# Attention, linear attention, LSTM and FP4 FFN in one kernel: another order of work in the first stage's steps

## Chip, cores and metric

The kernel runs on one core of one Trainium2 chip. The metric is device time in microseconds: before the change the median of three runs is 953.55 us (952.65 to 953.72).

## What is computed

The input x has 64 sequences of 64 rows of 256. The first stage computes x1 = x + attention part, the second x1 + FFN part:

```python
# first stage, per sequence
y  = softmax_attention([image key; k], [image value; v], q) @ c_proj   # 16 heads of 16, causal, one extra key
q2, k2, v2 = relu(y @ Wq.T + bq), relu(y @ Wk.T + bk), y @ Wv.T + bv
ctx = (q2 @ (k2.T @ v2)) / max(q2 @ sum(k2), 1e-6)                     # per head
x1  = x + layernorm(ctx + y) * gamma + beta
# second stage
hs  = lstm(x1, h0=cond, Wx, Wh, b)                                     # along the 64 rows
out = x1 + fp4_linear(silu(fp4_linear(hs, w_gate)) * fp4_linear(hs, w_up), w_down)
```

Most products are done as three f16 products of a high and a low part (high x high, high x low, low x high). So each operand of such a product is made twice: a cast on ScalarE gives the high part, and a subtraction on VectorE the low part.

## The kernel before

**Tiles and steps.** A tile is two sequences, 128 rows, so there are NT = 32 of them. The first stage is a software pipeline written out by hand: each engine has its own function `step`, and `pipeline` calls it with a list of tiles, the newest first (t1 = tile n, t2 = tile n-1, and so on). Step n of an engine does the early work of t1 and later work of t2 to t5. Steps 0 to 9 are written out, steps 10 to 29 are a loop of ten rounds with two steps each, and the rest is written out again. Each engine carries out its list in order; semaphores join them. The second stage (LSTM, FP4 products) follows from about 514 us on and is not changed.

**What a step does.** For t1: x's high and low part (of the tile after it), the q, k product (`qk`), the split of q and k into `qk16` (L1104 to L1107 on ScalarE, L1376 and L1377 on VectorE), their DMA transposes into `qkT` (L555), the scores of the first eight heads (`scores(t1, 0)`, L827) and the mask sum `masked(t1, 0)` (L1347). For t2: the scores of the other eight heads, row maxima (`maxima`, L1355), subtraction of them (`shift`, L651, GpSimd), exp (L1082), p's high part (L1088) and low part (`probs_lo`, L658), the image key's part (`image_part`, L667), and the transposes of p (`probs_turn`, L540). For t3: p times v (`attend`, L841), the sum of the parts and its division (L1387 to L1396), the transpose of the result (onT), the projection y (L1163), y's transpose and yT's high and low part (L1077, L1331). For t4: the linear attention (`linear_q`, `linear_kv`, `outer`, `linear_out`; L1403 to L1421), the residual (L711), and the statistics: `bn_stats` (L1445), `bn_aggr` (L1453), variance plus epsilon (L713) and rstd (L715). For t5: z (L1137), times gamma (L685), plus x and beta (L692) which gives x1, its high part (L1156) and low part (L1433), the DMA transposes of x1 (L574) and its store (L576).

**SyncE's queue.** All DMAs are issued from SyncE, in order. In a step these are: on even steps x_in for the next pair (L547); the two q, k transposes (L555); p's two transposes (L540); on even steps the image values of two tiles (L568, two issues of 136 KB); x1's transposes and store (L574, L576); on even steps x_res (L579). An issue whose source isn't ready holds up all behind it.

**VectorE's order.** A step begins with maxima of t2's first heads, then x's low part, the split of q and k, weight work in steps 0 to 8 (`chore`), the second mask sum and maxima of t2, the sum and division of t3, the head mask of t4 (L1403), onT's low part, ctx (L1421), v's low part (L1428), x1's low part (L1433), the mask sum of t1 (L1347), statistics of t4 (L1445), yT's low part (L1331), and the aggregation (L1453). In the last steps of the stage the weights of the FFN are split too (`ffn_hi`, `ffn_lo`, L483).

**Helpers.** `hold(engine, semaphore, value, passed)` waits and then increments a counter; `after` is a wait that is left out where its value isn't positive. All matrix products with three parts are on L783.

## Time and profile before

| | before |
|---|---|
| median of 3 runs | 953.55 us (952.65 to 953.72) |
| the profiled execution | 955.28 us, span 953.6 us |
| mean granted TensorE clock | 0.926 |
| TensorE (PE) busy | 766.9 us, 80% |
| VectorE (DVE) busy | 747.1 us, 78% |
| ScalarE (ACT) busy | 429.5 us, 45% |
| GpSimd (POOL) busy | 436.2 us, 46% |
| DMA, mean 93 GB/s | 89.04 MB, queue q1 46.7% of 16 engines |
| issue to landing, median: q, k transposes | 4.2 us |
| issue to landing, median: image values (32 issues of 136 KB) | 3.1 us |

The span runs from the first to the last instruction of the profiled execution, and the difference to 955.28 us lies around it. Busy shares are means over two stages with different limits; the page gives them in 40 slices of 23.8 us, of which slices 3 to 21 are about the first stage. A number in brackets behind a row of a timeline is the idle time of the engine before the operation, and what ended it.

### The profile page before, as it was taken

Reading aid. Unit: us, or ns where it says so; the run is one execution under the profiler, and the core shown is the slowest. Engines: PE = TensorE matmul, PEld = TensorE weight load, DVE = VectorE, ACT = ScalarE, POOL = GpSimd, SP = SyncE. Lnnn points to the kernel's source line nnn. Section 1 sums busy time; section 2 is a strip of 40 time slices with the busy share of each in tenths; the row PEclk is TensorE's granted clock in tenths of the full one; section 3 lists DMA queues with packets and bytes.
Section 4 is the critical chain, followed back from the end, with each engine's and each line's share of the span. In section 5 each row is a group of like instructions: output and inputs, shape, how many; then the busy total and the mean of one; then the engine's idle time right before and its main releaser. Section 6 shows DMA issues by size and latency. Waiting matters only on the chain.

```text
span 953.6 us, 23040 instructions
## 1 busy us (share of the span) xinstructions
PE 766.9 (80%) x7494; PEld 466.0 (49%) x7494; DVE 747.1 (78%) x1773; ACT 429.5 (45%) x1145; POOL 436.2 (46%) x596
## 2 busy tenths in 40 slices
PE   3347677778888778887767799999999999999965
PEld 1124454445455444554444455555555556555633
DVE  6177878667777778777744689999999999999883
ACT  2054656556665666665553333333333333333320
POOL 0054777666766667766742033322233333222332
PEclk9767989889998999999898999999999999999987
DMA  5965656676665666666620023323332333233332
GB/s 120 185 168 98 113 112 105 124 130 132 131 128 122 133 127 139 132 138 127 119 56 23 17 48 59 66 58 67 64 64 59 67 59 64 60 66 64 65 64 63
DMA packets 262383, 89.04 MB, mean 93 GB/s; under 512 B 233266, under 2 KB 261298, under 8 KB 262325
## 3 DMA queue, kind: packets, MB, share of 16 engines
q1 hardware_dynamic: 262324, 88.25, 46.7%
q8 instruction: 39, 0.64, 0.3%
q14 instruction: 20, 0.16, 0.1%
HBM read 25.19 MB, written 8.47 MB: 35 GB/s over the span
## 4 chain that ended last, share of the span: by engine, by line
PE 29%; DVE 17%; POOL 11%; issue 10%; SPq 9%; DMA 6%; ACT 4%; POOLq 0%; DVEq 0%; ACTq 0%
PE bank L783 10%; PE bank L920 8%; PE bank L931 5%; DVE x_value L170 4%; DMA qkT<-qk 4%; SPq L540 3%; POOL p L658 2%; DVE ffn_room L1530 2%; DVE ffn_room L1526 2%; POOL prob L651 2%; PE bank L1000 2%; PE bank L911 2%; POOL zg_rows L685 1%; SPq L568 1%; POOL x_rows_sb L692 1%
## 5 line engine op out<-in xcount | busy, mean ns | idle before, releaser
L783 PE MATMUL bank<-gu,xqT 128*128 128x512 f16 (+1 forms) x576 | 128.5, 371 | 8.6 <-DMA xqT<-xq_split 8.6
L729 POOL TENSOR_TENSOR ffn_room<-prob,h_coarse 128x704 f16<-128x704 f32 x32 | 44.1, 1377 | 154.4 <-DVE prob L171 154.4
L920 PE MATMUL bank<-wx,x1T 128*64 128x512 f16 x768 | 97.9, 392 | 2.9 <-DMA x1T<-x_split 2.9
L931 PE MATMUL bank<-wh,h 128*64 128x512 f16 x768 | 96.0, 386 | 0.7 <-ACT h L1190 0.7
L651 POOL TENSOR_TENSOR prob<-prob,row_max 128x520 f32<-128x520 f32 x64 | 68.8, 1075 | 50.7 <-DVE row_max L1355 50.7
L783 PEld LDWEIGHTS bank<-gu,xqT 128*128 128x128 f16 x576 | 56.2, 102 | 69.2 <-issue 12.2
L920 PEld LDWEIGHTS bank<-wx,x1T 128*64 128x64 f16 x768 | 79.4, 203 | 13.5 <-DMA x1T<-x_split 3.7
L1009 PE MATMUL bank<-dn,hqT 128*128 128x256 f16 x576 | 70.0, 277 | 7.6 <-DMA hqT<-ffn_room 6.6
L658 POOL TENSOR_TENSOR p<-prob,p 128x512 f16<-128x512 f32 x64 | 72.0, 1125 | 1.2 <-ACT p L1088 1.2
L1009 PEld LDWEIGHTS bank<-dn,hqT 128*128 128x128 f16 x576 | 54.7, 99 | 26.5 <-issue 18.3
L931 PEld LDWEIGHTS bank<-wh,h 128*64 128x64 f16 x768 | 41.5, 111 | 42.0 <-issue 12.1
L1347 DVE TENSOR_TENSOR prob<-bank,add_mask 128x260 f32<-128x260 f32 x128 | 48.4, 419 | 16.5 <-PE bank L827 16.2
L154 ACT ACTIVATE qk<-prob 128x704 bf16<-128x704 f32 x32 | 25.3, 792 | 75.5 <-DVE prob L167 75.5
L827 PE MATMUL bank<-qkT 64*64 64x65 f16 x1024 | 22.6, 211 | 45.7 <-DMA qkT<-qk 32.4
L783 PE MATMUL bank<-attn,xT 128*128 128x512 f16 x192 | 59.1, 454 | 0.0
L783 PE MATMUL bank<-yT,lin 128*128 128x128 f16 x384 | 31.1, 239 | 34.4 <-DVE yT L1331 34.4
L811 PE MATMUL bank<-attn,xT 128*64 128x256 f16 x768 | 56.8, 287 | 0.0
L1082 ACT ACTIVATE prob<-prob 128x520 f32<-128x520 f32 x64 | 40.7, 635 | 30.9 <-POOL prob L651 30.9
L724 POOL TENSOR_TENSOR h_coarse<-h_scale,one_h 128x44 bf16<-128x44 f32 x32 | 8.9, 279 | 98.3 <-DVE h_scale L165 98.3
L788 PE MATMUL bank<-bias_rows_sb,ones_bf 96*128 96x512 bf16 (+1 forms) x96 | 36.7, 383 | 18.3 <-DVE onT L1331 9.8
L783 PE MATMUL bank<-lin,yT 128*128 128x512 f16 x192 | 50.7, 403 | 0.0
L783 PEld LDWEIGHTS bank<-yT,lin 128*128 128x128 f16 x384 | 26.5, 109 | 48.3 <-DVE yT L1331 40.5
(193 smaller groups left out, 1869.5 us busy)
## 6 DMA issues: line engine op xcount, KB each, us to landing
vimg_in<-image_values SPq DMA_DIRECT2D x32, 136.0 KB, 3.1
x_in<-in_x_columns SPq DMA_DIRECT2D x16, 256.0 KB, 2.9
x_res<-in_x SPq DMA_DIRECT2D x16, 256.0 KB, 3.0
x_rows<-x_rows_sb SPq DMA_DIRECT2D x32, 128.0 KB, 1.8
ffn_room<-x_rows SPq DMA_DIRECT2D x64, 64.0 KB, 2.2
out<-ffn_room SPq DMA_DIRECT2D x64, 64.0 KB, 2.0
add_mask<-in_mask_Bx1x1xS_ff SPq DMA_DIRECT2D x2, 512.0 KB, 7.6
qkT<-qk SPq DMA_TRANSPOSE x64, 4.2
```

The lines of the kernel that those rows point to most:

```text
L170: 5: lambda: dve.scalar_tensor_tensor(out=v, in0=mag, scalar=1.25 * MAGIC, in1=v, op0=ALU.max, op1=ALU.subtract),
L651: pool.tensor_tensor(prob[:, r, :], prob[:, r, :], row_max[:, r, None].to_broadcast([P, 8, KEYS]), ALU.subtract).then_inc(s["shifted"], 1)
L658: pool.tensor_tensor(p16[:, r, 1, :], prob[:, r, 0:S], p16[:, r, 0, :], ALU.subtract).then_inc(s["p_lo"], 1)
L729: pool.tensor_tensor(blocks(hq_split[:, 0], FF), blocks(fp4_h.value, FF), spread(h_coarse, FF), ALU.mult).then_inc(s["hq_hi"], 1)
L783: last = pe.matmul(dst, lhs(a, c), rhs(b, c), start=first and c == 0 and a == b, stop=c == C - 1 and (a, b) == parts3[-1], skip_group_chec ...
L788: pe.matmul(dst, ones_bf[:, :], bias_bf[name][:, lo:hi], start=True, stop=False, skip_group_check=True)
L811: last = pe.matmul(bank[3][64 * copy:64 * copy + 64, D * h:D * h + D], xT16[:, t.parity, a, P * c + 64 * h:P * c + 64 * h + 64], attn16[:, ...
L920: last = pe.matmul(bank[e][B * h:B * h + B, :], x1T16[m][:, c, :, at], half_cols(wx16, a, c, h), start=False, stop=True, skip_group_check= ...
L931: last = pe.matmul(bank[e][B * h:B * h + B, :], h16[:, m, c, :], half_cols(wh16, a, c, h), start=False, stop=True, skip_group_check=True)
L1009: last = pe.matmul(dst, hqT16[:, t.parity, a, k, :], dn16[:, m, k, :], start=k == 0 and (a, m) == (0, 0), stop=k == FFC - 1 and a == 1, sk ...
L1082: act.activation(prob[:, r, :], prob[:, r, :], ACT.Exp, scale=1.0 / SCORE).then_inc(s["probs"], 1)
L1347: last = dve.tensor_tensor(prob[:, at:at + 4, :], bank[side][:, 0:4 * KEYS].rearrange("p (r k) -> p r k", k=KEYS), add_mask[:, bass.ds(t.n ...
```

## The change

All of it is in the first stage. The pipelines of VectorE and SyncE get a sixth tile, t6.

- SyncE: the image values go tile by tile (`image_values`, two issues of 68 KB a step in place of two of 136 KB on even steps) and stand first in the step; x_res is next (now for t4 of even steps), then x_in, then the q, k transposes, then x1's transposes and store (of t6), and last p's transposes.
- VectorE: yT's low part stands ahead of the mask sum of t1, and the maxima of that sum follow it in the same step (before: first thing of the next). Statistics come a step later (t5), behind x's low part, and the aggregation behind the split of q and k, with three counted waits (`passed`). x1's low part comes a step later (t6), behind the second maxima.
- GpSimd: variance and rstd (t5) stand behind the copy of the image keys; x1's sum (L692) stands behind p's low parts.
- ScalarE: onT's high part stands ahead of the second exp; x1's high part (L1156) behind yT's.

```diff
@@ SyncE
+        def image_values(t):
+            hold(sp, s["img_part"], t.count(2, 2, back=2), "sp_passed")
+            for b in range(2):
+                sp.dma_start(vimg_in[64 * b:64 * b + 64, t.parity].rearrange("p h c -> p (h c)"),
+                             vimg_sides[b][t.number()].partition_broadcast(S)).then_inc(vimg_loaded, 16)
         def step(tiles):
-            t1, t2, t3, _, t5 = tiles
+            t1, t2, _, t4, _, t6 = tiles
+            if t1 and (t1.loop is not None or t1.b > 0):
+                image_values(t1)
+            if t4 and t4.parity == 0:
+                after(sp, s["xb_ready"], t4.count(back=1))
+                sp.dma_start(x_res[:, :, :], x_pairs[t4.pair()]).then_inc(xres_loaded, 16)
...
-            if t2:
-                probs_turn(t2, 0)
-                probs_turn(t2, 1)
...
-                if t1.parity == 0:
-                    hold(sp, s["img_part"], t1.count(2, 2, back=1), "sp_passed")
-                    for b in range(2):
-                        sp.dma_start(vimg_in[64 * b:64 * b + 64, :].rearrange("p j h c -> p j (h c)"),
-                                     vimg_sides[b][bass.ds(t1.number(), 2)].partition_broadcast(S)).then_inc(vimg_loaded, 16)
...
-            if t5:
-                hold(sp, s["x1_lo"], t5.count(), "sp_passed")
+            if t6:
+                hold(sp, s["x1_lo"], t6.count(), "sp_passed")
...
-            if t3 and t3.parity == 0:
-                after(sp, s["xb_ready"], t3.count(back=1))
-                sp.dma_start(x_res[:, :, :], x_pairs[t3.pair()]).then_inc(xres_loaded, 16)
-        pipeline(sp, 5, step, first=10)
+            if t2:
+                probs_turn(t2, 0)
+                probs_turn(t2, 1)
+        pipeline(sp, 6, step, first=10)
@@ GpSimd
+            if t5:
+                pool.wait_ge(s["mean_ready"], t5.count())
+                after(pool, s["rstd_ready"], t5.count(back=1))
+                after(pool, s["z_ready"], t5.count(back=1))
+                pool.tensor_tensor(var_eps[:, :], mean_var[:, 1:2], eps_ln[:, :], ALU.add).then_inc(s["var_ready"], 1)
+                pool.wait_ge(s["var_ready"], t5.count())
+                pool.tensor_tensor(rstd[:, :], var_eps[:, :], neg_half[:, :], ALU.pow).then_inc(s["rstd_ready"], 1)
             if t2:
                 image_part(t2, 0)
                 shift(t2, 1)
...
                 pool.tensor_tensor(zg_rows[:, :], z_rows[:, :], gamma_sb[:, :], ALU.mult).then_inc(s["zg_ready"], 1)
+            if t2:
+                probs_lo(t2, 0)
+                image_part(t2, 1)
+                probs_lo(t2, 1)
             if t5:
...
                 pool.tensor_tensor(x1_rows[:, t5.parity, :], zg_rows[:, :], xb_rows[:, :], ALU.add).then_inc(s["x1_ready"], 1)
-            if t2:
-                probs_lo(t2, 0)
-                image_part(t2, 1)
-                probs_lo(t2, 1)
@@ ScalarE
                 probs_hi(t2, 0)
-                exp(t2, 1)
             if t3:
                 hi(t3, onT16[:, 0, :], bank[0][:, 0:D], "onT_ps", "onT_hi", "y_ps")
+            if t2:
+                exp(t2, 1)
@@ VectorE
+        def passed(sem, value):
+            hold(dve, sem, value, "dve_passed")
         def step(tiles):
-            t1, t2, t3, t4, t5 = tiles
+            t1, t2, t3, t4, t5, t6 = tiles
-            if t2:
-                maxima(t2, 0)
             if t1 and (t1.loop is not None or t1.b < NT - 1):
                 x_lo(Tile(t1.loop, t1.b + 1))
+            if t5:
+                dve.wait_ge(s["resid"], t5.count())
+                dve.bn_stats(stats[:, :], res_rows[:, :]).then_inc(s["stats_ready"], 1)
...
+            if t5:
+                passed(s["stats_ready"], t5.count())
+                passed(s["var_ready"], t5.count(back=1))
+                passed(s["neg_ready"], t5.count(back=1))
+                dve.bn_aggr(mean_var[:, :], stats[:, :]).then_inc(s["mean_ready"], 1)
             chore(t1, 0)
             if t2:
                 masked(t2, 1)
                 maxima(t2, 1)
+            if t6:
+                dve.wait_ge(s["x1_hi"], t6.count())
+                dve.tensor_tensor(x1_split[:, 1, :], x1_rows[:, t6.parity, :], x1_split[:, 0, :], ALU.subtract)\
+                    .then_inc(s["x1_lo"], 1)
...
-                masked(t1, 0)
-            if t4:
-                dve.wait_ge(s["resid"], t4.count())
-                dve.bn_stats(stats[:, :], res_rows[:, :]).then_inc(s["stats_ready"], 1)
...
             if t3:
                 lo(t3, yT16[:, 1, :], bank[6][:, D:2 * D], yT16[:, 0, :], "yT_hi", "yT_lo")
+            if t1:
+                masked(t1, 0)
+            if t1:
+                maxima(t1, 0)
             if t4:
-                dve.bn_aggr(mean_var[:, :], stats[:, :]).then_inc(s["mean_ready"], 1)
                 ffn_lo(t4, "mean")
```

## Rows read from the trace of the kernel before

**Rows 1.** By stretch: us (instructions) of PE, PEld, DVE, ACT, POOL; clock, DMA, GB/s

```profile
322.00:348.00 26.00, 20.86 (x283) 13.04 (x283) 19.89 (x54) 16.11 (x42) 17.91 (x27) 0.93 0.64 131
```

**Rows 2.** SyncE's queue: start, us, line, operation, what; q, k issues, steps 3, 10, 31

```profile
82.93 1.29 SPq L555 DMA_TRANSPOSE qkT<-qk  x1
...
188.15 3.34 SPq L555 DMA_TRANSPOSE qkT<-qk  x2
...
462.80 3.04 SPq L555 DMA_TRANSPOSE qkT<-qk  x2
```

**Rows 3.** SyncE's queue over one pair of steps

```profile
308.91 3.02 SPq L555 DMA_TRANSPOSE qkT<-qk  x2
...
320.44 3.19 SPq L555 DMA_TRANSPOSE qkT<-qk  x2
326.83 2.87 SPq L540 DMA_TRANSPOSE pT<-p  x2
330.00 1.49 SPq L568 DMA_DIRECT2D vimg_in<-image_values  x2
331.80 1.23 SPq L574 DMA_TRANSPOSE x1T<-x_split  x1
333.22 0.44 SPq L576 DMA_DIRECT2D x_rows<-x_rows_sb  x1
333.94 0.40 SPq L579 DMA_DIRECT2D x_res<-in_x  x1
334.67 1.29 SPq L555 DMA_TRANSPOSE qkT<-qk  x1
```

**Rows 4.** VectorE in order of time, same pair; in brackets idle time before, and releaser

```profile
319.75 0.41 DVE L1377 TENSOR_TENSOR qk<-bank,qk 128x256 f16<-128x256 f32 x1
...
321.48 0.44 DVE L1387 TENSOR_TENSOR bank<-bank,o_img 128x272 f32<-128x272 f32 x1
...
326.98 1.35 DVE L1433 TENSOR_TENSOR x_split<-x_rows_sb,x_split 128x256 f16<-128x256 f32 x1
...
329.63 0.43 DVE L1445 BATCH_NORM_STATS2 stats<-res_rows 128x6 f32<-128x256 f32 x1 [0.62 <-POOL res_rows L711]
330.09 0.42 DVE L1331 TENSOR_TENSOR yT<-bank,yT 128x256 f16<-128x256 f32 x1
...
331.43 0.42 DVE L1376 TENSOR_TENSOR qk<-bank,qk 128x256 f16<-128x256 f32 x1
...
332.09 0.76 DVE L1347 TENSOR_TENSOR prob<-bank,add_mask 128x260 f32<-128x260 f32 x2
332.88 0.69 DVE L1355 TENSOR_REDUCE row_max<-prob 128x8 f32<-128x520 f32 x1
333.50 0.45 DVE L1387 TENSOR_TENSOR bank<-bank,o_img 128x272 f32<-128x272 f32 x1
```

**Rows 5.** TensorE in order of time, same pair of steps

```profile
315.03 0.44 PE L827 MATMUL bank<-qkT 64*64 64x65 f16 x16 [2.32 <-DMA qkT<-qk]
...
326.49 0.32 PE L827 MATMUL bank<-qkT 64*64 64x65 f16 x16
327.04 0.44 PE L849 MATMUL bank<-ident,y_rows 128*128 128x128 f32 x2 [0.23 <-ACT y_rows L1163]
...
330.57 0.84 PE L783 MATMUL bank<-yT,lin 128*128 128x128 f16 x12 [1.58 <-DVE yT L1331]
```

**Rows 6.** GpSimd in order of time: the low part of p beside x1's low part

```profile
326.93 1.12 POOL L658 TENSOR_TENSOR p<-prob,p 128x512 f16<-128x512 f32 x1
```

**Rows 7.** VectorE and GpSimd in step 31, the other order of starts

```profile
467.50 0.44 DVE L1433 TENSOR_TENSOR x_split<-x_rows_sb,x_split 128x256 f16<-128x256 f32 x1
...
467.62 1.30 POOL L658 TENSOR_TENSOR p<-prob,p 128x512 f16<-128x512 f32 x1
```

**Rows 8.** VectorE at the stage's end: the last weight splits

```profile
509.61 0.95 DVE L483 SCALAR_TENSOR_TENSOR gu<-bank,gu 128x512 f16<-128x512 f32 x2
```

**Rows 9.** p's transposes (L540): time from issue to landing over the whole trace

```profile
DMA to landing us min/median/max: 3.0/3.2/4.8
```

More of the change, by code:

```diff
@@ L1164, in step @@
                 hi(t3, yT16[:, 0, :], bank[6][:, D:2 * D], "yT_ps", "yT_hi", "kv2_ps")
+            if t5:
+                act.wait_ge(s["x1_ready"], t5.count())
+                after(act, s["x1T_in"], t5.count(per=16, nth=16, back=1))
+                act.copy(x1_split[:, 0, :], x1_rows[:, t5.parity, :]).then_inc(s["x1_hi"], 1)
             ffn_hi(t4, "mean")
@@ L1460, in _ @@
         x_lo(Tile(None, 0))
-        pipeline(dve, 5, step, first=10)
+        pipeline(dve, 6, step, first=10)
         dve.memset(hq_split[:, :, FF:], 0.0).then_inc(s["b_zero"], 1)
```

27 lines of the change are left out of this document (6 added, 21 removed).

## The prediction

> **What bounds the kernel now.** I read the page first (busy shares by slice), then the busy times by stretch, then SyncE's DMA queue in order of time, then VectorE, TensorE, GpSimd and ScalarE over the same two steps. In the steady part of the first stage no engine is full: in 26 us TensorE works 20.9, VectorE 19.9, GpSimd 17.9, ScalarE 16.1 [rows 1]. What counts is the waits that end last. The second stage (from 514 us on) is not touched and keeps its time.
>
> A step handles one new tile and older ones behind it. Steps come in pairs, since x_in and x_res move two tiles at once. From the q, k transposes issued at 188.15 us (step 10) to those at 462.80 us (step 31) there are 21 steps in 274.65 us [rows 2]: 26.16 us a pair. In the pair shown they go out at 308.91, 320.44 and 334.67 us [rows 3]: 11.53 and 14.23 us apart. I call the issue at 320.44 that of an even step, those at 308.91 and 334.67 odd. Two waits stand out:
>
> Wait one, the queue. In the long step q and k are split from 331.43 us on, 0.66 us from there to the next operation [rows 4], so they are ready at about 332.2, but the transposes leave at 334.67: SyncE first issues p's transposes, the image values, x1's transposes, x1's store and x_res [rows 3]. 2.5 us late. In the same place a pair earlier the lateness shows as TensorE idle: the scores at 315.03 waited 2.32 us for qkT [rows 5].
>
> Wait two, yT's low part. TensorE waits 1.58 us for it before 330.57; y's transposes were done by 327.5 [rows 5]. VectorE is first busy with x1's low part (1.35 us) and the mask sum and then sits 0.62 us idle ahead of the statistics, which wait for GpSimd's residual [rows 4].
>
> **The change part by part.** A "gap" is start to start on one engine. I write s for the start of the scores of the new tile's first half on TensorE (326.49 in the even step) and run one step of the new order from it.
>
> (a) yT's low part first. y's transposes begin at s+0.55 and take 0.44 [rows 5]; ScalarE's cast behind them I take at 0.4, as VectorE's operation on the same tile has 0.42 [rows 4]. Low part at s+1.45. Linear q can then start right behind the next q, k product: wait two is gone. Price: the mask sum begins about 1 us after its scores, not at once.
>
> (b) VectorE from there: yT's low part 0.34 (the two operations of the split, of the same size, have gaps of 0.33), mask sum 0.79, maxima 0.62, x's low part 0.34, statistics 0.46, split done 0.75 later [rows 4]: s+4.75. The statistics' residual was made a step before, so the 0.62 us of idleness has no cause left. SyncE issues 0.28 us after the split (319.75+0.41 to 320.44) [rows 3, 4]: s+5.0.
>
> (c) From that issue to the scores it takes 315.03-308.91 = 6.12 us [rows 3, 5]. **Loop one**: 5.0+6.1 = 11.1 us a step.
>
> (d) x1's low part comes a step later, behind the second maxima. It takes 1.35 us [rows 4] where GpSimd's p low part started 0.05 us before it, and it ends 0.28 after that one's end [rows 6]; 0.44 where it started first, with GpSimd's at 1.30 in place of 1.12 [rows 6, 7]. In the new place the operation behind the maxima starts 0.62 us after their start [rows 4], GpSimd's subtraction only after their end at 0.69 plus a semaphore: VectorE should be first by some 0.1 to 0.2 us. I take a gap of 0.34; bounds 0.34 and 1.35.
> The Trainium skill (SBUF — State Buffer, Who interferes with whom) says that a VectorE instruction with two inputs in SBUF and a GpSimd one that reads SBUF exclude each other for the whole instruction, the first to start having it. The rows named before this agree; by this rule the part is unhindered when first, and when second it waits out GpSimd's whole subtraction.
>
> (e) **Loop two**: split 0.66 from s+4.0, aggregation 0.2 (estimate, a tiny operation), second mask sum 0.79, maxima 0.62, x1's part 0.34 put the sum with the image part at s+6.6. From that operation to the next scores it is 326.49-321.48 = 5.0 us now [rows 4, 5], less 0 to 0.5 because onT's high part no longer stands behind an exp on ScalarE: 11.1 to 11.6, I take 11.35. VectorE is then close to full: 19.9/2 us [rows 1] less about 1 for x1's part leaves it 9 to 10 of 11.4.
>
> (f) The three "passed" counters ahead of the aggregation are waits that are met, each with an increment. SyncE has three like them in the 0.33 us between x_res's end and the q, k issue [rows 3]: so 0 to 0.3 us here, taken as inside the 11.35.
>
> (g) SyncE's queue, by gaps [rows 3]: x1's transposes 1.42, its store 0.72, p's 3.17, image values 1.80, x_res 0.73, x_in taken alike, q, k transposes 3.3 (3.19 and a semaphore). The image values go from two issues a pair to four, of half the bytes. Bytes seem to count little (two of 136 KB take 1.49, one x_res of 256 KB 0.40), so I take 1.80 again; bounds 1.0 and 1.8. Odd step 3.3+1.42+0.72+3.17+1.80 = 10.4 us, below the loops. Even step 10.4+1.46 = 11.9, above them: this is what is late next. Behind the waits: x_in waits for x's low part (s+3.2) with q and k behind it, which want s+5.0: no loss. x1's transposes wait for x1's low part, done at s+6.6, 1.6 us after the q, k issue and before its 3.3 us are over: no loss. p's are now last, 5.4 us behind the q, k issue.
>
> (h) GpSimd: variance and rstd move from the step's end, where they waited for the aggregation, to its middle; x1's sum goes behind p's low parts, so these come about 0.9 us sooner. rstd again waits for the aggregation (s+4.9), with the image part and second subtraction behind it; these want an exp and the maxima of about s+5 and s+5.9: hidden, 0.5 if not. The residual ends near s+13.4 (estimate) and is wanted a step later at s+14.5: 1 us to spare.
>
> (i) ScalarE: onT's high part ahead of the second exp delays that exp by 0 to 0.4 us, off both loops. x1's high part fits behind yT's.
>
> **Sum.** A pair is 11.9 (queue) + 11.35 (loop two) = 23.25 for 26.16: 2.91 us, times 10.5 pairs = 30.6 us. The steps from 3 to 10 (82.93 to 188.15 us, 15.0 each [rows 2]) hold weight work on VectorE beside the same two waits: between 0 and 7x1.45 = 10, taken as 5. Tail: 0 to 5 saved on the same yT wait, but the last tile's statistics and low part now stand behind weight splits like the one of 0.95 us [rows 8], with ScalarE's high part ahead of it: 2.8 lost at most; 1 saved on balance. Together 36.6. The profiled execution took 955.28 us (span 953.6), 1.73 above the median: 955.28-36.6 = 918.7, less 1.7 is 917.
>
> **The rivals.**
> 1. x1's low part loses the race of (d): 1.35 in place of 0.44 makes loop two 12.26 in both steps, the pair 24.5, saved 17.3+6 = 23: **930 us**. For: that collision is the rule now [rows 6]. Against: the order of starts in (d). Chance 0.17.
> 2. p's transposes, last in the queue, become the wait. The second is issued at about s+11.6 and lands 3.2 us later, s+14.8; TensorE wants it at about the same moment. Landings go up to 4.8 [rows 9]. If each step is late by 1.2, the pair is 25.6, saved 6+5: **943 us**. Chance 0.14.
> 3. Slower: the queue stalls at x1's transposes. They now stand ahead of p's, and their source is on VectorE behind the second mask sum. Each microsecond by which x1's low part ends later than 3.3 us after the q, k issue moves p's transposes, attend, o, y and the next scores. The slack is 1.7 us and the gain 1.45 us a step, so from 3.2 us of lateness it is a loss; 0.3 us beyond, over 28 steps, gives **962 us**. For: in the early steps weight work stands right ahead of it. Against: the steady steps have nothing there. Chance 0.06.
> 4. It does nothing: both waits only hid a third limit, such as the DMA engines, already 0.64 busy [rows 1]. **953 us**. Chance 0.04.
> The forecast itself (900 to 928) has 0.55. Better than 900 (image issues at half their price, both loops at 10.9) has 0.04.
>
> **How the numbers follow.** Likeliest: 917. Left out are rivals 3 and 4 (0.10), below 900 (0.04) and the far part of rival 2 (0.05): 900 to 940. This kernel's measurement can tell about 0.2% (1.9 us) from no change. Faster 0.90, within 0.04, slower 0.06.
>
> **What would show it.** Right: no wait of linear q for yT; q, k transposes 0.3 us behind the split in odd steps and behind x_in in even ones; x1's low part 0.44 long; pairs of 23 us; TensorE waiting under 1 us for qkT. Wrong: image issues dearer than 0.75 each, attend released by p's landing, statistics waiting for the residual, or TensorE's granted clock at its lower level for more of the stage than now.

## The result, and the profile after

The changed kernel takes 925.84 us (median of 4 runs, 924.49 to 930.52) where the kernel before takes 953.17 in the same comparison: a ratio of 0.9722, 95% interval 0.9687 to 0.9757. The prediction was 917, with a range of 900 to 940. The profiled execution took 926.43 us, span 924.7, where I had put 918.7.

By stretch, first the changed kernel's steady steps (they answer rows 1) and its steps 4 to 9 (columns as in rows 1):

```profile
306.00:332.00 26.00, 22.79 (x321) 14.89 (x321) 20.45 (x63) 19.41 (x49) 20.14 (x29) 1.00 0.77 149
...
100.00:187.00 87.00, 64.72 (x774) 41.77 (x775) 65.41 (x167) 47.84 (x118) 68.12 (x77) 0.82 0.56 110
```

The same view of the kernel before, steps 4 to 9:

```profile
100.00:187.00 87.00, 61.63 (x780) 38.54 (x784) 67.00 (x167) 49.07 (x119) 64.44 (x78) 0.90 0.61 114
```

In the steady steps TensorE is busier (22.8 of 26 us, not 20.9), and its granted clock is 1.00, not 0.93. In steps 4 to 9 the clock went the other way, from 0.90 to 0.82. That is the first sign that the two parts of the stage fared differently. The sum of the prediction has no term for the clock in either.

SyncE's queue of the changed kernel: the q, k transposes of steps 3, 10 and 31 (for rows 2), with the pair of steps that answers rows 3 between them:

```profile
82.12 3.04 SPq L567 DMA_TRANSPOSE qkT<-qk  x2
...
187.91 3.36 SPq L567 DMA_TRANSPOSE qkT<-qk  x2
...
310.24 2.66 SPq L540 DMA_TRANSPOSE pT<-p  x2
313.16 1.20 SPq L546 DMA_DIRECT2D vimg_in<-image_values  x2
314.62 0.40 SPq L555 DMA_DIRECT2D x_res<-in_x  x1
315.37 3.24 SPq L567 DMA_TRANSPOSE qkT<-qk  x2
318.89 1.61 SPq L577 DMA_TRANSPOSE x1T<-x_split  x1
320.69 0.42 SPq L579 DMA_DIRECT2D x_rows<-x_rows_sb  x1
321.38 2.65 SPq L540 DMA_TRANSPOSE pT<-p  x2
324.80 1.30 SPq L546 DMA_DIRECT2D vimg_in<-image_values  x2
326.40 0.40 SPq L559 DMA_DIRECT2D x_in<-in_x_columns  x1
327.22 3.17 SPq L567 DMA_TRANSPOSE qkT<-qk  x2
...
429.39 3.09 SPq L567 DMA_TRANSPOSE qkT<-qk  x2
```

From these issues the span's difference of 28.9 us is accounted for. "Tail" runs from step 31's issue to the first product of the second stage.

| us | before | after | saved | predicted |
|---|---|---|---|---|
| up to step 10 | 188.15 | 187.91 | 0.2 | 5 |
| steps 10 to 31 | 274.65 | 241.48 | 33.2 | 30.6 |
| tail | 49.27 | 52.74 | -3.5 | 1 (with the second stage) |
| second stage | 441.53 | 442.57 | -1.0 | |

VectorE of the changed kernel over one step, in order of time (for rows 4):

```profile
311.37 0.42 DVE L1338 TENSOR_TENSOR yT<-bank,yT 128x256 f16<-128x256 f32 x1 [1.38 <-ACT yT L1083]
311.73 0.77 DVE L1354 TENSOR_TENSOR prob<-bank,add_mask 128x260 f32<-128x260 f32 x2
...
313.47 0.42 DVE L1383 BATCH_NORM_STATS2 stats<-res_rows 128x6 f32<-128x256 f32 x1
...
314.13 0.41 DVE L1389 TENSOR_TENSOR qk<-bank,qk 128x256 f16<-128x256 f32 x1
...
315.93 0.42 DVE L1403 TENSOR_TENSOR x_split<-x_rows_sb,x_split 128x256 f16<-128x256 f32 x1
316.26 0.44 DVE L1409 TENSOR_TENSOR bank<-bank,o_img 128x272 f32<-128x272 f32 x1
...
325.23 0.41 DVE L1389 TENSOR_TENSOR qk<-bank,qk 128x256 f16<-128x256 f32 x1
```

TensorE of the changed kernel, same steps (for rows 5; L833 are scores, L847 attend, L789 the linear products):

```profile
310.24 0.32 PE L833 MATMUL bank<-qkT 64*64 64x65 f16 x16 [1.02 <-DMA qkT<-qk]
...
312.28 0.83 PE L789 MATMUL bank<-yT,lin 128*128 128x128 f16 x12
...
314.87 0.43 PE L847 MATMUL bank<-v,pT 128*64 128x34 f16 x16 [0.80 <-DMA pT<-p]
...
321.35 0.32 PE L833 MATMUL bank<-qkT 64*64 64x65 f16 x16 [0.21 <-issue]
...
333.43 0.32 PE L833 MATMUL bank<-qkT 64*64 64x65 f16 x16 [1.18 <-DMA qkT<-qk]
```

The wait of linear q for yT is gone (312.28 carries no bracket; it was 1.58 us in rows 5), and the statistics at 313.47 no longer wait. From the scores at 310.24 to those at 321.35 it is 11.11 us, with no wait for a transfer at the end. From there to 333.43 it is 12.08, and that step ends in a wait of 1.18 us for qkT: q and k were split at 325.64, and their transposes went out at 327.22, behind the image values and x_in.

### The profile page after: what moved, and what is told of

It reads as the page before. It is cut to its first block, busy times and chain, and to the rows that moved or that the text cites. A ratio compares the mean times of both kernels' runs of the same rounds, so it can differ in the third digit from the quotient of the medians.

```text
span 924.7 us, 23230 instructions
## 1 busy us (share of the span) xinstructions
PE 759.0 (82%) x7494; PEld 466.1 (50%) x7494; DVE 727.7 (79%) x1773; ACT 431.9 (47%) x1145; POOL 439.3 (48%) x596
## 4 chain that ended last, share of the span: by engine, by line
PE 27%; SPq 23%; DVE 18%; issue 7%; DMA 3%; ACT 2%; POOL 1%; DVEq 0%; ACTq 0%; POOLq 0%
PE bank L926 9%; PE bank L789 8%; SPq L567 7%; SPq L540 5%; PE bank L937 5%; DVE x_value L170 4%; SPq L577 4%; DVE ffn_room L1542 3%; DVE ffn_room L1538 2%; SPq L546 2%; PE bank L1006 2%; PE bank L917 2%; DVE fc L1480 1%; DVE x_value L171 1%; ACT x_magnet L154 1%
## 5 line engine op out<-in xcount | busy, mean ns | idle before, releaser
L789 PE MATMUL bank<-gu,xqT 128*128 128x512 f16 (+1 forms) x576 | 127.7, 369 | 7.4 <-DMA xqT<-xq_split 7.4
L654 POOL TENSOR_TENSOR prob<-prob,row_max 128x520 f32<-128x520 f32 x64 | 74.0, 1157 | 70.7 <-DVE row_max L1362 70.0
L789 PEld LDWEIGHTS bank<-gu,xqT 128*128 128x128 f16 x576 | 56.0, 102 | 67.2 <-issue 12.3
L1015 PEld LDWEIGHTS bank<-dn,hqT 128*128 128x128 f16 x576 | 54.7, 99 | 26.7 <-issue 18.3
L817 PE MATMUL bank<-attn,xT 128*64 128x256 f16 x768 | 61.0, 302 | 0.0
L817 PEld LDWEIGHTS bank<-attn,xT 128*64 128x64 f16 x768 | 41.0, 120 | 21.8 <-issue 20.0
L789 PE MATMUL bank<-attn,xT 128*128 128x512 f16 x192 | 51.8, 410 | 0.0
L833 PE MATMUL bank<-qkT 64*64 64x65 f16 x1024 | 21.2, 202 | 35.5 <-DMA qkT<-qk 22.2
L789 PE MATMUL bank<-lin,yT 128*128 128x512 f16 x192 | 48.7, 391 | 0.0
L741 POOL TENSOR_TENSOR xq<-x_value,x_scale 128x256 f32<-128x256 f32 x32 | 19.8, 620 | 58.5 <-DVE x_value L171 58.5
L1193 ACT ACTIVATE bank<-cell 128x128 f32<-128x128 f32 x64 | 18.0, 281 | 60.7 <-DVE cell L1484 60.7
```

Source lines behind the costliest of these rows:

```text
L654: pool.tensor_tensor(prob[:, r, :], prob[:, r, :], row_max[:, r, None].to_broadcast([P, 8, KEYS]), ALU.subtract).then_inc(s["shifted"], 1)
L789: last = pe.matmul(dst, lhs(a, c), rhs(b, c), start=first and c == 0 and a == b, stop=c == C - 1 and (a, b) == parts3[-1], skip_group_chec ...
L817: last = pe.matmul(bank[3][64 * copy:64 * copy + 64, D * h:D * h + D], xT16[:, t.parity, a, P * c + 64 * h:P * c + 64 * h + 64], attn16[:, ...
L1015: last = pe.matmul(dst, hqT16[:, t.parity, a, k, :], dn16[:, m, k, :], start=k == 0 and (a, m) == (0, 0), stop=k == FFC - 1 and a == 1, sk ...
```

## The experiments

All times are medians of 4 runs (6 in experiments 4, 5 and 11). Ratios, with their 95% intervals, go against runs of the kernel before on the same chip, whose medians lie between 952.8 and 954.1 us; they are estimated over all the runs and differ by up to 0.002 from the quotient of the two medians. A "turn" is one step of the pipeline. "Steady" is from the q, k issue of step 10 to that of step 31, from the profile: 274.65 us before, 241.48 after.

**1. The queue alone.** The engines of before with the new order of SyncE, x1's transposes a turn later among it, and the image values by tile.

```diff
+                image_values(t1)
...
+            if t6:
+                hold(sp, s["x1_lo"], t6.count(), "sp_passed")
...
+            if t2:
+                probs_turn(t2, 0)
```

> The kernel before with the new order of SyncE's queue alone: image values by tile, x_res and x_in first, then q and k, then x1's transposes and store of the tile whose low part is from the step before, p's transposes last. The engines keep their old order. My theory: two waits, one of 2.3 us a pair at the q, k transposes and one of 1.58 us a step at yT's low part, are separate. This takes the first away and leaves the second: both steps of a pair become like the short one, about 11.8 us, the pair 23.8 for 26.16, and the early steps gain nothing: 953.2 - 25 = 928 us (922 to 936). The rival, that one of the two waits only shows the other (a common limit), expects little: above 945 us.

Measured: 936.26 us (932.91 to 937.32), ratio 0.9809 (0.9782 to 0.9837), steady 252.4. This is 0.3 us above the range expected. It is three fifths of the whole gain by the medians, seven tenths by the ratios.

**2. The engines alone.** The changed engines with the queue of before; only the tile of x1's transposes is a turn later, as it must be.

```diff
-            if t5:
-                hold(sp, s["x1_lo"], t5.count(), "sp_passed")
+            if t6:
+                hold(sp, s["x1_lo"], t6.count(), "sp_passed")
```

> The changed kernel with the old order of SyncE's queue (x_in, q and k, p, the image values of two tiles, x1 and its store, x_res), all engines in their new order. My theory: the queue then sets the pair: from p's second low part, about 11.8 us behind the scores of the new tile, come 1.6 for p's second transposes, 1.8 + 1.42 + 0.72 + 0.73 for what stands before q and k, 6.1 to the scores two tiles on: 24.3 us a pair for 26.16, and the tail costs the 4.5 us that it costs in the changed kernel: 953.2 - 19.5 + 4.5 = 938 us (930 to 946). If the new order of the engines were worth nothing without the queue it would be 950 or more; if it were all of the gain, 926.

Measured: 1004.22 us (1003.24 to 1006.29), ratio 1.0536 (1.0510 to 1.0563). My expectation was wrong in sign. The rows tell why, SyncE's queue first:

```profile
343.91 3.24 SPq L555 DMA_TRANSPOSE qkT<-qk  x2
348.60 3.53 SPq L540 DMA_TRANSPOSE pT<-p  x2
352.50 1.51 SPq L568 DMA_DIRECT2D vimg_in<-image_values  x2
354.33 1.22 SPq L574 DMA_TRANSPOSE x1T<-x_split  x1
```

ScalarE of the same kernel (x1's high part):

```profile
357.08 0.41 ACT L1168 CAST x_split<-x_rows_sb 128x256 f16<-128x256 f32 x1 [5.76 <-DMA x1T<-x_split]
```

and TensorE, which needs v from ScalarE:

```profile
360.99 0.59 PE L880 MATMUL bank<-v,k 64*128 64x130 f32 x2 [3.94 <-ACT v L1130]
```

x1's split has one buffer. Its high part for the next tile waits until the transposes of the last one have read it. They now belong to a tile of a turn earlier but still stand last in the queue, so they go out late in the step, and ScalarE is held for 5.76 us with xT, q, k and v behind. That is the wait of every second step; between 230 and 425 us ScalarE waited 13 times in this place, 47.6 us in all.

**3. The same, x1's transposes ahead of p's.** Two issues move; nothing else differs from experiment 2.

```diff
+            if t6:
+                hold(sp, s["x1_lo"], t6.count(), "sp_passed")
...
             if t2:
                 probs_turn(t2, 0)
                 probs_turn(t2, 1)
...
-            if t6:
```

> The changed engines (VectorE, ScalarE, GpSimd) with the queue of the kernel before, as in the run at 1004 us, but with x1's transposes and x1's store ahead of p's transposes instead of behind them and the image values; nothing else of the queue is the new one. Theory: in the run at 1004 us x1's high part on ScalarE (one buffer for one tile) waited 5.76 us for the transposes of the tile before, issued at 354.33 behind q,k, p and the 136 KB of image values; everything behind it on ScalarE came late, and TensorE waited 3.94 us for v. With the transposes ahead of p they start some 5 us earlier, and the wait goes: 29 us per pair of steps become 23.3 to 24.5, 925 to 945 us, taken 932. Rival one: what cost the time was the place of q,k behind the 256 KB of x_in, or the image values in one issue of 136 KB; then the time stays above 980 us. Rival two: x1's transposes now hold p's, and TensorE's wait moves to p: 950 to 975 us.

Measured: 923.93 us (921.33 to 927.57), ratio 0.9692 (0.9655 to 0.9729), steady 236.5. The time is 1 us below the range expected. The cause is shown: with the changed engines, this one place in the queue is worth 80 us, and ScalarE's high part of x1 no longer waits for the transposes between 230 and 425 us. The kernel also has the whole effect of the change, with the image values still in pairs, and with them, x_in and x_res where they stood before: its ratio can't be told from that of the changed kernel.

**4. x1's transposes alone.** The kernel before, with x1's transposes and store a turn later and ahead of p's: the queue's edits of 2 and 3 together, and no engine is changed.

> The kernel before with one edit: x1's transposes and x1's store are issued a turn later, behind q,k's transposes and ahead of p's, instead of behind p's and the image values in their own turn. Every engine and the rest of SyncE's queue are as before. Theory: this one move is what the whole new queue brought in the run at 936 us, since SyncE no longer stands before x1's low part while the next step's q,k are due (in the kernel before that wait holds q,k back every step); q,k's place ahead of x_in's and the image values by tile add nothing: 933 to 939 us, taken 936. Rival one: the image values by tile and the image and residual loads ahead of q,k carry the gain: 945 to 953 us. Rival two: ScalarE's x1 high part, which waits for the transposes of the tile before, now comes late, as in the run at 1004 us: over 955 us.

Measured: 938.88 us (936.66 to 943.38), ratio 0.9832 (0.9781 to 0.9883), steady 253.2. It can't be told from the effect of the whole new queue (0.9809), as expected. The reason given in the expectation doesn't stand, though: in the kernel before, SyncE did not wait for x1's low part. That part was done at 328.33 us, and the transposes went out at 331.80, right behind the image values. What the queue of before waited for, between 230 and 425 us (us in total, times, longest), is p:

```profile
SPq L462 <- POOL p L658: 27.6, 15, 3.8
```

It stood idle from the end of the q, k issues (323.63) to p's at 326.83, and then had p's, the image values, x1's two and x_res ahead of the next q and k. In experiment 4 x1's two issues fill that idle time: the waits for p fall to 2.8 us, and q, k's transposes go out at 321.18, 0.3 us behind their split, where they were 2.5 us late. TensorE's waits for qkT in this stretch fall from 16.3 us to 0.4; those for yT stay (12.1 and 11.8).

**5. The same, and x1's low part a turn later on VectorE.**

```diff
+            if t6:
+                dve.wait_ge(s["x1_hi"], t6.count())
...
             if t3:
                 dve.wait_ge(s["o_copied"], t3.count())
```

> The same, and in addition VectorE's low part of x1 a turn later, in front of the attention's sum, where the changed kernel has it; all else as before. Theory (step d of the prediction): its 0.85 us mean beside GpSimd's work (0.98 at 315.36 in the run with the new queue alone) falls to 0.42, and it no longer stands between v's low part and the mask sum, ahead of yT's low part, for which TensorE waits 0.96 us in every second step: 0.4 to 0.9 us a step, 10.5 pairs, 5 to 12 us, so 925 to 931 us, taken 928. Rival: the low part's place is worth nothing by itself, since VectorE then waits for the mask sum or the residual instead, and the gain over the queue alone comes from the order of yT, statistics and maxima: 933 to 938 us.

Measured: 936.49 us (933.70 to 940.32), ratio 0.9806 (0.9755 to 0.9856), steady 251.7. The rival was right. VectorE of this kernel:

```profile
310.22 0.56 DVE L1386 TENSOR_TENSOR x_split<-x_rows_sb,x_split 128x256 f16<-128x256 f32 x1
...
315.93 0.76 DVE L1347 TENSOR_TENSOR prob<-bank,add_mask 128x260 f32<-128x260 f32 x2
318.12 0.43 DVE L1445 BATCH_NORM_STATS2 stats<-res_rows 128x6 f32<-128x256 f32 x1 [1.43 <-POOL res_rows L711]
318.58 0.43 DVE L1331 TENSOR_TENSOR yT<-bank,yT 128x256 f16<-128x256 f32 x1
```

and of the one before it, without that edit:

```profile
316.13 0.88 DVE L1433 TENSOR_TENSOR x_split<-x_rows_sb,x_split 128x256 f16<-128x256 f32 x1 [0.38 <-ACT x_split L1156]
316.93 0.75 DVE L1347 TENSOR_TENSOR prob<-bank,add_mask 128x260 f32<-128x260 f32 x2
318.31 0.43 DVE L1445 BATCH_NORM_STATS2 stats<-res_rows 128x6 f32<-128x256 f32 x1 [0.63 <-POOL res_rows L711]
```

The q, k issues before these rows went out at 309.24 and 309.25, so the times can be compared. x1's part became shorter (0.56 for 0.88 us), the mask sum starts 1.0 us sooner, and the statistics then wait 1.43 us for the residual in place of 0.63: yT's low part starts 0.19 us sooner (318.58 for 318.77). The remaining 15 us of steady time to experiment 3 come from what is left: statistics a turn later, yT ahead, and the orders on GpSimd and ScalarE.

**6. x1's low part late.** The changed kernel, with x1's low part a turn later still behind v's low part, so that x1's transposes, ahead of p's in the queue, wait.

```diff
-            if t6:
-                dve.wait_ge(s["x1_hi"], t6.count())
...
                                   v16[:, t1.parity, :, 0, :, 0:HD], ALU.subtract).then_inc(s["v_lo"], 1)
+            if t6:
+                dve.wait_ge(s["x1_hi"], t6.count())
```

> The changed kernel with x1's low part at VectorE's place behind v's low part, where VectorE has 0.6 to 1.5 us of idleness in front of yT's low part, in place of right behind the second maxima. For VectorE's own time this is free or better. My theory (rival 3 of the prediction): x1's transposes stand ahead of p's in SyncE's queue and now wait for it, some 4 us longer. A loop closes: x1's low part, x1's transposes and store 2.3, p's second transposes 1.6 + 3.2 to landing, attend, sum and division, back to v's low part 5.6 and x1's 1.3: about 14.9 us a step for 11.5, 21 steps: 926 + 71 = 997 us (980 to 1010), and TensorE waits for pT by 3 us a step. If the place in the queue doesn't matter: 926 us. The low part itself I expect at 1.35 us again, beside GpSimd's p low part or x1 sum.

Measured: 1068.98 us (1068.31 to 1070.61), ratio 1.1218 (1.1192 to 1.1244). Right in direction, low by 72 us. Its queue:

```profile
335.45 3.24 SPq L567 DMA_TRANSPOSE qkT<-qk  x2
344.66 1.20 SPq L577 DMA_TRANSPOSE x1T<-x_split  x1
...
346.81 2.66 SPq L540 DMA_TRANSPOSE pT<-p  x2
```

The queue stands still for 6.0 us (338.69 to 344.66) in front of x1's low part, and TensorE waits 3.96 us for p further on. Steps take 17.1 us in place of 11.5: the stall passes into the step nearly one for one, and TensorE's granted clock is 0.80 between 250 and 440 us, where the changed kernel has 1.00 between 250 and 425. This is rival 3 of the prediction, with its mechanism. Here x1's low part is done at 344.43 (it starts at 343.58 and takes 0.85), 5.7 us after q, k's transposes were issued; in the changed kernel at 316.35, 2.3 us before (318.61).

**7. yT's low part behind mask sum and maxima.** The change's first item undone.

```diff
-            if t3:
-                lo(t3, yT16[:, 1, :], bank[6][:, D:2 * D], yT16[:, 0, :], "yT_hi", "yT_lo")
             if t1:
                 masked(t1, 0)
             if t1:
                 maxima(t1, 0)
+            if t3:
+                lo(t3, yT16[:, 1, :], bank[6][:, D:2 * D], yT16[:, 0, :], "yT_hi", "yT_lo")
```

> The changed kernel with one pair undone: the mask sum and maxima of the new tile ahead of yT's low part on VectorE. My theory: yT's low part is not ready when the mask sum could run (VectorE waits 0.6 to 1.5 us for it now), so the mask sum starts 1 us sooner and yT's low part comes 0.5 to 1 us later, at s+2.0 in place of s+1.2; TensorE wants it at s+2.1. So nearly the same, the 1.4 us of both together hide in TensorE's q, k product: 926 us within 4 us. That says the gain of the title's first part comes from x1's low part and the statistics having left that place, not from the swap with the mask sum. The rival, that the swap itself carries wait two, expects about 1.5 us a step: 926 + 30 = 956 us.

Measured: 927.40 us (926.74 to 929.86), ratio 0.9726 (0.9705 to 0.9746). By itself the item named first in the change is worth nothing that can be measured, as expected. TensorE waits 0.32 us for yT in every second step. So what had made that wait 1.58 us was the work around it, x1's part ahead of it and the statistics' wait. Of the two, x1's part has been moved alone: between 230 and 425 us TensorE's waits for yT fell from 11.8 us (experiment 4) to 7.5 (experiment 5). The statistics have not.

**8. Image values issued by ScalarE.** The changed kernel, with the two issues taken out of SyncE's queue; they count on two semaphores, one for each parity of the tile, in place of one.

```diff
-            if t1 and (t1.loop is not None or t1.b > 0):
-                image_values(t1)
...
                 act.copy(by_bank(o_sum[:, :, :]), o_part(1, HD)).then_inc(s["o_copied"], 1)
+            if t1 and (t1.loop is not None or t1.b > 0):
+                image_values(act, "act_passed", t1)
```

> The changed kernel with the image values issued by ScalarE, behind its copy of the attention's sum, instead of by SyncE. In the changed kernel SyncE's queue has no gap over 0.4 us in steady steps: 23.14 us from p's transposes at 310.24 to those two steps on at 333.38, of which the image values take 1.20 and 1.30 and their gaps 0.26 to 0.38. Theory (the queue is the bound of the steady step): without them it needs 20.1 us for a pair, and the next bound, loop one at 11.1 us, decides: 22.2 to 22.6 us for a pair instead of 23.1, 6 to 10 us in all, 916 to 920 us, taken 918. Rival one (the queue follows the engines and only looks full): 925 to 927 us. Rival two: the two issues hold ScalarE, the exponentials come later, and p with them: 930 to 945 us.

Measured: 920.96 us (918.06 to 923.42), ratio 0.9640 (0.9606 to 0.9674), steady 235.7, or 22.4 us a pair in place of 23.0. That is 1 us above the range expected, and its interval lies clear of the changed kernel's. So the queue does bound the step in part: 0.55 us a pair. Freeing 3.1 us of it gives no more, so something else comes next. (The queue was not quite without gaps, as the expectation has it: there are 0.77 us ahead of the issue at 324.80.) TensorE of this kernel, between 230 and 425 us (us in total, times, longest):

```profile
PE bank L845 <- DMA pT<-p: 11.2, 21, 1.1
```

**9. The weight work of steps 3 to 10 elsewhere.** The changed kernel; VectorE's part behind v's low part, ScalarE's a step later and behind its copy of the attention's sum (not shown), and one scaling a step later.

```diff
-    SCALE_AT = {1: "down", 3: "gate", 5: "up"}
+    SCALE_AT = {1: "down", 3: "gate", 6: "up"}
...
-            chore(t1, 0)
+            if t1 and t1.loop is None and t1.b < 3:
+                chore(t1, 0)
...
+            if t1 and t1.loop is None and t1.b >= 3:
+                chore(t1, 0)
```

> The changed kernel with the weight work of steps 3 to 10 in another place: VectorE's part behind the low part of v instead of behind the split of q,k, ScalarE's part a step later and behind its copy of the attention's sum, and one scaling a step later. In the changed kernel TensorE waits for the attention's rows 3.32, 4.88, 3.32, 2.90, 4.18 and 1.20 us in steps 3 to 9, since VectorE's weight work of 2.7 to 4 us stands inside the path from q,k over the statistics and the maxima to the attention's sum; VectorE then idles 1.56 and 1.58 us later in the step. Theory (this is where the predicted 5 us of the early steps went): half or more of the 19.8 us comes back, steps 3 to 10 take 95 to 99 us instead of 105.8, and the time is 915 to 920 us, taken 918. Rival one: the work only moves into the path over yT and the scores, which is as tight: 924 to 929 us. Rival two: the early steps are bound by the queue's weight transposes, and nothing on VectorE changes them: 925 to 927 us.

Measured: 923.15 us (918.89 to 925.46), ratio 0.9658 (0.9620 to 0.9696); steps 3 to 10 took 103.17 us in place of 105.79. That is less than expected, and by itself it shows no gain: the intervals of the two ratios overlap, and experiment 10, in which these steps are those of the changed kernel, took 103.56 for them. TensorE's waits between 80 and 190 us mostly moved: 21.9 us for the attention's rows in the changed kernel,

```profile
PE bank L855 <- DVE o_rows L1418: 21.9, 7, 4.9
```

and 13.9 us for yT in this one, with 1.6 left for the attention's rows:

```profile
PE bank L789 <- DVE yT L1341: 13.9, 6, 4.0
```

**10. The tail's order.** The changed kernel, with the means' weight splits behind the last aggregation and the last one behind x1's last low part.

```diff
                 dve.bn_aggr(mean_var[:, :], stats[:, :]).then_inc(s["mean_ready"], 1)
+                ffn_lo(t5, "mean")
...
-            if t4:
-                ffn_lo(t4, "mean")
```

> The changed kernel with the low parts of the feed-forward weights' means ahead of the next turn's work on VectorE behind the last aggregation, and the last unit behind the last x1 low part, so that they no longer stand ahead of the last tile's statistics and x1's low part. In the changed kernel the statistics of the last tile start at 472.74, right behind four such operations (1.90 us each way of the row at 470.92), and the last x1 low part at 479.17, behind one of 0.96 us; TensorE then waits 7.55 us for x1's transposes. Theory: the wait shrinks by 2 to 3 us and the time with it: 922 to 924.5 us, taken 923.5. Rival: the clock of the first recurrent stage stays low for as much longer as the wait is shorter, or the weights come late instead: 926 to 928 us. This also measures the tail, which the prediction costed at +1 and the result at -3.5.

Measured: 924.99 us (918.81 to 927.78), ratio 0.9702 (0.9675 to 0.9729). In the median it can't be told from the changed kernel, and it is 0.5 us above the range expected. The profile, which is of the fastest of the four runs, shows the mechanism: the tail took 48.76 us in place of 52.74, and the wait before the first recurrent product 3.07 in place of 7.55. The two kernels of experiment 11, which have this edit, also wait 3.07 there.

**11. Two together, and three together.** Experiment 3 with both edits of 9 and 10; and the changed kernel with those of 8, 9 and 10.

> The kernel of the run at 923.9 us (changed engines, queue of before with x1's transposes ahead of p's), with the tail's order (means' low parts behind the last aggregation) and the weight work of steps 3 to 10 moved as in the runs that tried each. If the gains add: 923.9 less 3 (tail 52.74 to 48.76 in the profile, about 1 in the median) less 2.6 (steps 3 to 10 took 103.17 instead of 105.79) gives 918, range 915 to 922. Rival: the clock of the recurrent stage takes the tail's part back, and the steps 3 to 10, which are at 103.47 here without it, give nothing more: 922 to 925 us.

> The changed kernel with all three: image values issued by ScalarE (921.0 us alone), the tail's order (925.0 alone) and the weight work moved (923.2 alone), against 925.8 for the changed kernel. If the gains add: 925.8 less 4.9, 0.9 and 2.7 gives 917.3, range 913 to 920. Rival: in the steps of the weight work SyncE's queue of weight transposes sets the step once VectorE no longer does, and the two gains there are one: 919 to 922 us.

Measured: 912.63 us (910.71 to 915.23), ratio 0.9559 (0.9512 to 0.9607), and 913.37 us (910.74 to 914.60), ratio 0.9563 (0.9515 to 0.9611). The first is below its expected range (915 to 922), the second inside its own. Both beat the changed kernel by 1.6 to 1.7% by the ratios, 1.4% by the medians. In medians that is more than the single gains add up to (13.2 us for 5.5, and 12.5 for 8.4); by the ratios it is so for the first only (1.6 points for 1.1), and not beyond the intervals. In the first, steps 3 to 10 took 99.1 us (103.5 in experiment 3), the tail 50.3 (53.9) and the second stage 441.2 (443.1); in the second, steps 3 to 10 took 100.4 (104.9 in experiment 8). Here the weight work's new place does show, in both. TensorE's waits between 80 and 190 us hardly differ between experiment 3 and the first kernel (24.1 and 23.9 us in all), but its granted clock between 100 and 187 us is 0.92 in place of 0.82. The two kernels are equal, so the old order of the queue with x1's transposes ahead of p's does as well as the new one with the image values off it. ScalarE's image issues on top of the old order were not tried. The kernel to keep is the first: it needs fewer edits to the queue than the change itself.

## Why the prediction was right or wrong, point by point

The total was right in sign and 8.8 us too good. In the profiled execution the error is 7.7 us (926.43 against 918.7): steady steps 2.6 better, the part up to step 10 4.8 worse, tail and second stage 5.5 worse. The other 1.1 is the step from that execution to the median: 1.7 was taken off, and the changed kernel's median lies 0.6 below its profiled execution.

The steady steps come out near in size (33.2 us saved for 30.6), but not as two waits that can be taken away one by one: the new queue alone gives 17 us, x1's transposes alone give 14, and the new engines alone lose 51. The image values by tile and the places of x_res and x_in in front, which the queue's sum counts, are not needed for it (experiment 3). The granted clock of the steady steps, 1.00 for 0.93, is part of the 33.2 us too; how much was not separated, and the sum had no term for it. That the size fits is partly luck.

**(a), (b)** right: yT's low part at s+1.1 (s+1.45 predicted), the split done at s+4.30 in both steps (s+4.75 predicted). That yT goes *first* isn't what removed wait two (experiment 7); the prediction credited the place and should have credited the removed neighbours, which it named too.

**(c)** right: from issue to scores 5.98 and 6.21 us (6.12 predicted). Where the queue lets it, the step is 11.11 us, as loop one had it.

**(d)** right: x1's part takes 0.42 us in the new place, 0.88 to 1.35 in the old one. GpSimd's subtraction beside it (L654) has a mean of 1.16 us, against 1.08 before (L651). The Trainium skill (SBUF — State Buffer, Who interferes with whom) has the later one of such a pair wait for the earlier, and the trace agrees in direction: 0.08 us went to GpSimd. But by rival 1 the longer part would have cost 13.6 us (36.6 saved against 23). Moved alone, in experiment 5, the part brought 2.4 us, between kernels whose intervals overlap.

**(e)** mis-sized, by little: the sum with the image part begins at s+6.02, not s+6.6, and the next scores come 5.09 us later. Loop two is 11.11 us and not 11.35.

**(f)** right: the aggregation starts 0.33 us behind the split's second operation; the counters don't show.

**(g)** the total was right and its parts weren't. Start to start, x1's transposes took 1.80 and 1.93 us (1.42 predicted), the image values 1.46 and 1.60 (1.80 at the upper bound), x_in or x_res 0.75 and 0.82 (0.73). And x_in and x_res don't fall into the same step, as the prediction had it: x_res goes at 314.62 and x_in at 326.40. So every step has one of them, and the q, k issues are 11.2 and 11.85 us apart, where the queue was predicted to need 10.4 and 11.9. Pairs of 23.0 us (23.25 predicted) come out well since the longer step is the queue's in both accounts. Of the two lateness figures, 0.83 us of the first (314.54 to 315.37) costs nothing, and 1.58 of the second costs 0.97.

**(h)** right, with less to spare: the residual ends at 324.25, and the statistics want it at 324.57.

**(i)** right: the second exp starts 0.27 us behind onT's cast (319.07 and 319.34), and x1's high part stands behind yT's, where it waits 0.34 us for its sum in every second step.

**The sum, steps 3 to 10.** This is the first step that failed: 5 us taken, -0.6 measured. (The same steps took 103.6 to 105.8 us over the four profiled kernels that have them as the change does or differ from it only in yT's place or the image issues, so the gain is between -0.6 and 1.7, and not 5.) As before the change, VectorE has the weight work between q, k's split and the second mask sum, and behind those the attention's sum. VectorE of the changed kernel in such a step:

```profile
112.96 1.76 DVE L170 SCALAR_TENSOR_TENSOR ffn_room<-hqT,ffn_room 128x1536 f32<-128x1536 bf16 x1
114.76 1.76 DVE L171 SCALAR_TENSOR_TENSOR ffn_room<-hqT,ffn_room 128x1536 f32<-128x1536 bf16 x1
116.43 0.76 DVE L1354 TENSOR_TENSOR prob<-bank,add_mask 128x260 f32<-128x260 f32 x2
```

TensorE, same step:

```profile
119.88 0.66 PE L855 MATMUL bank<-ident,o_rows 128*128 128x128 f32 x2 [4.88 <-DVE o_rows L1418]
120.47 1.49 PE L817 MATMUL bank<-attn,xT 128*64 128x256 f16 x12
```

In the kernel before TensorE waits in the same place:

```profile
119.34 0.41 PE L849 MATMUL bank<-ident,o_rows 128*128 128x128 f32 x2 [3.70 <-DVE o_rows L1396]
```

So the wait was there already, and it got longer, 4.88 for 3.70 us here, and 21.9 for 15.4 in all between 80 and 190 us. The waits for yT beside it (10.3 us in all before) went. Behind the longer wait the products run at the lower clock (1.49 us where L817 takes 0.85 in steady steps): the stretch's clock is 0.82 for 0.90, and TensorE is busy for 64.7 us of the 87 in place of 61.6. What the waits gave, the slower products took. "Between 0 and 10, taken as 5" had no row that put VectorE's weight work on the path; experiment 11 shows, at 4.4 and 4.5 us, that part of it is.

**The tail** is the second: 1 saved on balance, 3.5 lost. VectorE of the changed kernel there:

```profile
470.92 1.90 DVE L483 SCALAR_TENSOR_TENSOR gu<-bank,gu 128x512 f16<-128x512 f32 x4
472.74 0.42 DVE L1383 BATCH_NORM_STATS2 stats<-res_rows 128x6 f32<-128x256 f32 x1
...
478.29 0.96 DVE L483 SCALAR_TENSOR_TENSOR gu<-bank,gu 128x512 f16<-128x512 f32 x2 [4.26 <-ACT gu L1101]
479.17 0.42 DVE L1403 TENSOR_TENSOR x_split<-x_rows_sb,x_split 128x256 f16<-128x256 f32 x1
```

and TensorE's first recurrent product:

```profile
482.13 2.85 PE L926 MATMUL bank<-wx,x1T 128*64 128x512 f16 x12 [7.55 <-DMA x1T<-x_split]
```

In the kernel before:

```profile
512.07 2.35 PE L920 MATMUL bank<-wx,x1T 128*64 128x512 f16 x12 [2.86 <-DMA x1T<-x_split]
```

The wait is 4.7 us longer, where the prediction had 2.8 at most. It had seen one split of 0.95 us ahead of the statistics; there are two such pairs (1.90), and another of 0.96 ahead of the last low part. With the splits out of the way it is 3.07 (experiments 10 and 11), so their place is its cause. The gain of up to 5 set against it did not come. Nor is the wait all of the tail: in experiments 1 and 4, where the splits stand as before and the wait is 2.87 and 4.36, the tail took 54.6 and 54.7 us. Two reasons are at hand and neither was tested: x1's transposes come a turn later at the end, and step 31's q, k issue, from which the tail is counted, no longer comes late. The prediction had a term for neither. The second stage's -1.0 has no cause in the change: with the same code it took 441.2 to 446.8 us over the profiled executions.

**The rivals.** Rival 1 did not come (d). Rival 2's wait is there in part: between 100 and 440 us TensorE waited 31 times for p, 17.6 us in all, 0.6 each; landing takes 3.3 us in the median, 4.8 at most (rows 9: 3.2, 4.8). Rival 3 was shown to be real as a mechanism (experiment 6), and its slack held in the steady steps (2.3 us to spare). Rival 4 fell. What no part of the prediction had is the condition that carries it all: with the changed engines, x1's transposes must go ahead of p's, because ScalarE waits for them to use the one buffer of x1's split again (experiments 2 and 3; a second buffer was not tried). It looked at their wait for x1's low part only, and not at who waits for them.

**The signs.** Of those named as right, x1's low part (0.42), linear q without a wait and pairs of 23 us came. Two did not quite: the q, k transposes are 0.8 us behind their split and not 0.3 in the step that x_res is issued in, and TensorE still waits up to 1.7 us for qkT (12.4 us, 11 times, between 100 and 440 us). Of those named as wrong, p's landing releases attend, the dearer pair of image issues is 0.80 each, and the clock is lower in steps 4 to 9; none of them undid the gain.

**Open.** Which of the remaining engine edits (the statistics a turn later, GpSimd's and ScalarE's orders) brings the last 15 us of experiments 5 to 3 was not separated. Nor is it settled what bounds the pair at 22.5 and 22.4 us in experiments 3 and 8: two loops of 11.11 us would make 22.2, but TensorE also waits up to 1.1 us for p in each step there.

## What to carry to other kernels

When a transfer is moved in a queue, ask two things: what its source waits for, and which engine waits to reuse its buffer. Here the second was worth 80 us. Where several waits lie side by side, single trials show little (14 us for the transposes, 2 more for x1's part) and all the edits together show 29; undoing one from the full version shows what it is still worth there, which for yT was nothing. Look at where a queue stands idle: issues that fit into that time cost little there, as x1's did. Cost the start and the end of a stage step by step from their own rows: here they gave back a tenth of what the steady steps gained, and the prediction had counted on 6 us from them.

## What the runs showed of the hardware

- An issue's time on SyncE's queue depends on what is ahead. x1's transposes took 1.2 us where the queue had been idle for 6 us (344.66 in experiment 6) and also 0.3 us behind the image values (354.33 in experiment 2), but 1.6 to 1.7 right behind q, k's (318.89 and 330.71 in the changed kernel). Two image issues took 1.2 to 1.3 us for 68 KB each and 1.5 for 136 KB each: half the bytes are far from half the time.
- TensorE's granted clock fell where its waits were long, though not by their length alone. In steady steps with no wait over 1.4 us the clock was 1.00; with waits of 3 to 5 us in the steps it was 0.82 (steps 4 to 9) and 0.80 (experiment 6), and in experiment 6 the same linear product took 2.77 us for 1.46. In the same steps 4 to 9 it was 0.90 in the kernel before, with waits of up to 3.8 us, and 0.92 in the first kernel of experiment 11, with waits of up to 3.9. So a longer wait can cost more than itself, which no term of my sum had.
- Two issues in a row on ScalarE's queue took 1.66 us in experiment 8 (at 311.31), beside 1.2 to 1.3 on SyncE's. They held ScalarE a little: its next operation, which the profile has waiting for TensorE, started at 313.07, 0.5 us after the end of the product that it reads (312.61).
